# Sorted experts, two tiles at a time: shared PSUM banks for turned tiles and outputs, and twelve input places in place of sixteen

## The reference, cut to what matters

```python
for e in range(8):
    h = silu(flat @ W1[e]) * (flat @ W3[e])      # 128 -> 256
    out = out + cw[:, e:e + 1] * (h @ W2[e])     # 256 -> 128
```

## Time and profile before

| what | us |
|---|---|
| median of 3 runs | 2025.1 (2020.3 to 2026.32) |
| profiled execution, its own time | 2022.03 |
| span of its instructions | 2020.2 |
| m stage, from 1580 to 1718 | 138 |
| f stage, from 1853 to 1992 | 139 |

### The profile page before, as it was taken

One profiled execution on the slowest core, in us unless ns is written; L12 is line 12 of the kernel. 1 busy time (PEld: TensorE's weight loads), 2 busy tenths in 40 slices (PEclk: granted clock), 3 DMA queues, 4 the chain that ended last, 5 costly groups with the idle time before them and its releaser, 6 DMA issues. The chain is left out here.

```text
span 2020.2 us, 46758 instructions
## 1 busy us (share of the span) xinstructions
PE 1589.0 (79%) x16783; PEld 1166.6 (58%) x16783; DVE 1134.8 (56%) x3048; ACT 843.1 (42%) x1634; POOL 563.1 (28%) x782
## 2 busy tenths in 40 slices
PE   5788999999488879699988687898887597343992
PEld 3655666666266647478875454555554587332882
DVE  5745677777544447356544576876773343542433
ACT  2322455555211115344423254655553575001763
POOL 4111011111111103433202211133333355364554
PEclk9989799999699989899998886988896799555996
DMA  4000222221099200000001002222220242221224
GB/s 172 1 2 9 65 56 61 54 55 43 12 298 323 78 0 1 1 4 3 3 3 64 1 1 63 66 68 67 67 67 19 73 115 75 79 62 43 78 78 143
DMA packets 84683, 124.99 MB, mean 62 GB/s; under 512 B 17328, under 2 KB 70576, under 8 KB 82928
## 3 DMA queue, kind: packets, MB, share of 16 engines
q1 hardware_dynamic: 75824, 104.30, 17.7%
q0 software_dynamic: 8640, 17.78, 2.5%
HBM read 67.47 MB, written 55.59 MB: 61 GB/s over the span
## 5 line engine op out<-in xcount | busy, mean ns | idle before, releaser
L1527 DVE TENSOR_REDUCE small<-ps 128x8 f32<-128x1024 f32 (+1 forms) x256 | 312.6, 1223 | 122.6 <-PE ps L1313 70.4
L1454 ACT ACTIVATE scr<-ps 128x1024 f32<-128x1024 f32 x256 | 262.0, 1023 | 239.7 <-PE ps L1288 121.4
L244 POOL TENSOR_TENSOR rstd<-vare,neghalf 128x4 f32<-128x4 f32 (+1 forms) x72 | 63.2, 878 | 544.9 <-DVE vare L223 544.5
L2826 POOL DMA_INDIRECT results<-scr x142 | 135.9, 957 | 143.6 <-DVE scr L2815 59.0
L1326 PE MATMUL ps<-scr 128*32 128x256 f32 x2048 | 175.1, 417 | 0.2 <-ACT scr L1454 0.2
L1275 PEld LDWEIGHTS ps<-scr_r 32*128 32x128 f32 x1024 | 82.7, 196 | 153.3 <-ACT scr L1454 84.1
L1275 PE MATMUL ps<-scr_r 32*128 32x256 f32 x1024 | 137.0, 346 | 32.2 <-ACT scr L1454 18.4
L2746 PE MATMUL ps<-scr 128*128 128x128 f32 x1136 | 153.6, 279 | 1.3 <-ACT scr L2773 1.3
L1306 PE MATMUL ps<-scr_r 32*128 32x256 f32 x1024 | 138.6, 353 | 9.9 <-DMA scr_r<-scr_r 5.4
L2746 PEld LDWEIGHTS ps<-scr 128*128 128x128 f32 x1136 | 141.9, 196 | 1.6 <-issue 1.6
L1911 PE MATMUL ps<-scr 64*64 64x64 f32 x4480 | 120.8, 223 | 14.7 <-DVE scr L2201 7.0
(11 more groups left out here) (410 smaller groups left out, 3542.0 us busy)
## 6 DMA issues: line engine op xcount, KB each, us to landing
scr_r<-scr_r SPq DMA_DIRECT2D x512, 64.0 KB
rows_m<-kinds SPq DMA_DIRECT2D x8, 2064.0 KB, 30.3
rows_f<-kinds SPq DMA_DIRECT2D x8, 2064.0 KB, 74.3
scr<-results SPq DMA_DIRECT2D x32, 256.0 KB
scr<-rows_m SPq DMA_DIRECT2D x71, 64.5 KB
scr<-rows_f SPq DMA_DIRECT2D x71, 64.5 KB
scr<-in_l3m SPq DMA_DIRECT2D x1, 3072.0 KB, 9.9
results<-scr POOLq DMA_INDIRECT x142
```

Source lines behind the costliest of these rows:

```text
L244: pool.tensor_tensor(k.rstd[:, 0:self.J], k.vare[:, 0:self.J], k.neghalf[:, 0:self.J], ALU.pow).then_inc(self.e["rstd_ready"].sem, 1)
L1454: act.activation(PT[:, g % 2, 2 * x:2 * x + 2, :], ps[:, 4:6, :], ACT.Exp).then_inc(e["prob_ready"].sem, 1)
L1527: dve.tensor_reduce(nf[:, half, 0:blocks, at:at + 2].rearrange("p q a -> p a q"), ps[:, 2 * (p % 2):2 * (p % 2) + 2, :].rearrange("p a (q ...
L2826: pool.indirect_dma_start(results, bass.IndirectOffsetOnAxis(ap=names[:, j % IN, P:P + 1], axis=0), y[:, j % OUT, :], None).then_inc(store ...
```

## The change

Tiles 2m and 2m+1 form pair m. Turned tiles of a pair lie side by side in one bank (two banks), and ACT copies both by one instruction. Outputs of a pair lie side by side in one bank (two banks), and DVE copies both by one instruction. The products get four banks in place of three. `xT` and `y` get eight places in place of four. `xin` gets twelve places (`IN`) in place of sixteen. PE turns tile j+5 in step j in place of j+4. DVE copies pair m out behind the multiply of tile 2m+4, and POOL's two scatters of a pair wait for that copy.

```diff
-    IN, OUT, DEEP = 16, 4, 4
+    IN, XT, DEEP, OUT = 12, 8, 4, 8
     def turned_at(j):
-        return ps[:, j % 3, 0:P]
+        return ps[:, j // 2 % 2, P * (j % 2):P * (j % 2) + P]
     def hidden_at(j):
-        return ps[:, 3 + j % 3, :]
+        return ps[:, 2 + j % 4, :]
     def out_at(j):
-        return ps[:, 6 + j % 2, 0:P]
+        return ps[:, 6 + j // 2 % 2, P * (j % 2):P * (j % 2) + P]
     def sp(sp):
...
-            wait(sp, "turned", j - IN)
+            if there(j - IN):
+                wait_pair(sp, "turned", (j - IN) // 2)
             landed(sp, j - IN)
             arrived(sp, j - 4)
         def turn(j):
             arrived(pe, j)
-            wait(pe, "xt_ready", j - 3)
+            if j % 2 == 0:
+                wait_pair(pe, "xt_ready", j // 2 - 2)
...
         def gate_up(j):
-            wait(pe, "h_ready", j - 3)
+            wait(pe, "h_ready", j - 4)
...
         def project(j):
-            wait(pe, "out_read", j - 2)
+            if j % 2 == 0:
+                wait_pair(pe, "out_read", j // 2 - 2)
...
-        for j in range(-4, SORTED + 3):
+        for j in range(-5, SORTED + 3):
             if there(j):
                 gate_up(j)
-            if there(j + 4):
-                turn(j + 4)
+            if there(j + 5):
+                turn(j + 5)
             if there(j - 3):
                 project(j - 3)
...
+        def write_out(m):
+            wait(dve, "out_ready", tiles_of(m).stop - 1)
+            for j in range(2 * m - OUT, 2 * m - OUT + 2):
+                landed(dve, j)
+            out = ps[:, 6 + m % 2, 0:width(m)].rearrange("p (n c) -> p n c", c=P)
...
+        for j in range(SORTED + 5):
+            if ends_pair(j - 4):
+                write_out((j - 4) // 2)
             if there(j):
                 wait(dve, "act_ready", j)
...
-            wait(pool, "out_read", j)
+            wait_pair(pool, "out_read", j // 2)
             landed(pool, j - 4)
```

More of the change, by code:

```diff
@@ L2700, in wait, with wait_pair @@
             eng.wait_ge(e[name].sem, e[name].at(j))
+    def wait_pair(eng, name, m):
+        if 0 <= m:
+            eng.wait_ge(pairs[name].sem, pairs[name].at(m))
     def landed(eng, j):
@@ L2708, in arrived, with ends_pair, tiles_of, width @@
             eng.wait_ge(loads[j % 4].sem, loads[j % 4].at(j // 4))
+    def ends_pair(j):
+        return there(j) and (j % 2 == 1 or j == SORTED - 1)
+    def tiles_of(m):
+        return slice(2 * m, min(2 * m + 2, SORTED))
+    def width(m):
+        return P * (tiles_of(m).stop - 2 * m)
     def turned_at(j):
-        return ps[:, j % 3, 0:P]
+        return ps[:, j // 2 % 2, P * (j % 2):P * (j % 2) + P]
     def hidden_at(j):
-        return ps[:, 3 + j % 3, :]
+        return ps[:, 2 + j % 4, :]
     def out_at(j):
-        return ps[:, 6 + j % 2, 0:P]
+        return ps[:, 6 + j // 2 % 2, P * (j % 2):P * (j % 2) + P]
     def sp(sp):
@@ L2746, in gate_up @@
                     ins = pe.matmul(hidden_at(j)[:, 256 * n + P * c:256 * n + P * c + P],
-                                    here[:, j % DEEP, n, P * c:P * c + P], xT[:, j % DEEP, :], start=True, stop=True)
+                                    here[:, j % DEEP, n, P * c:P * c + P], xT[:, j % XT, :], start=True, stop=True)
             ins.then_inc(e["gu_ready"].sem, 1)
@@ L2773, in keep_weights, with keep_turned @@
             act.activation(here[:, j % DEEP], gate_up_of[:, :, bass.ds(at, 256)], ACT.Copy).then_inc(e["kept"].sem, 1)
-        def keep_turned(j):
-            wait(act, "turned", j)
-            wait(act, "gu_ready", j - DEEP)
+        def keep_turned(m):
+            wait_pair(act, "turned", m)
+            wait(act, "gu_ready", 2 * m + 1 - XT)
+            dst = xT[:, 2 * m % XT:2 * m % XT + width(m) // P, :].rearrange("p n c -> p (n c)")
+            src = ps[:, m % 2, 0:width(m)]
             if affine:
-                ins = act.activation(xT[:, j % DEEP, :], turned_at(j), ACT.Identity, scale=affine[0], bias=affine[1])
+                ins = act.activation(dst, src, ACT.Identity, scale=affine[0], bias=affine[1])
             else:
-                ins = act.activation(xT[:, j % DEEP, :], turned_at(j), ACT.Copy)
-            ins.then_inc(e["xt_ready"].sem, 1)
-        for j in range(-3, SORTED):
+                ins = act.activation(dst, src, ACT.Copy)
+            ins.then_inc(pairs["xt_ready"].sem, 1)
+        for j in range(-4, SORTED):
             if j == 2:
@@ L2788, in act @@
                 d.gap_exps(act)
-            if there(j + 3):
-                keep_turned(j + 3)
+            if ends_pair(j + 4):
+                keep_turned((j + 4) // 2)
             if there(j):
@@ L2799, in dve @@
         d.shift(dve)
-        for j in range(SORTED + 3):
+        def write_out(m):
[3 more added lines that the diff above has]
+            out = ps[:, 6 + m % 2, 0:width(m)].rearrange("p (n c) -> p n c", c=P)
+            dst = y[:, 2 * m % OUT:2 * m % OUT + width(m) // P, :]
+            if scale is None:
+                ins = dve.tensor_copy(dst, out)
+            else:
+                ins = dve.tensor_tensor(dst, out, row4(scale, width(m) // P), ALU.mult)
+            ins.then_inc(pairs["out_read"].sem, 1)
+        for j in range(SORTED + 5):
             if j == 4:
@@ L2809, in dve @@
                                   ALU.mult).then_inc(e["h_ready"].sem, 1)
[L2810 to L2818, removed]
             if beside and j < TILES:
@@ L2827, in pool @@
                                     y[:, j % OUT, :], None).then_inc(stores[j % 4].sem, 16)
-        for j in range(SORTED - OUT, SORTED):
+        for j in range(SORTED - 4, SORTED):
             landed(pool, j)
```

13 lines of the change are left out of this document (8 added, 5 removed).

## The result

The changed kernel takes 2116.5 us (median of 4 runs, 2095.3 to 2123.8), the kernel before beside it 2025.7 (4 runs, 2020.3 to 2029.4). The ratio is 1.043, with a 95% interval of 1.039 to 1.047. The direction was right. The size was not: 2062 was predicted, and 2116 lies above the range of 2038 to 2091.

The account below looks back on a forecast made before the run. No engine was full; PE's stall at the projection, then SP's loads, set the pitch. Twelve places at 1.94 us per tile added 18.5 (f) and 20.6 (m), 39 us on 2022.0: 2061, stated as 2062, range 2038 to 2091.

Parts of the forecast that it names:

- The mechanism: Both stages: twelve input places return too late, at 1.84 to 2.1 us per tile, 2041 to 2084 us; chance 0.70.
- Rival 2: Both stages: places are no limit, pairs remove PE's stall at the projection, 25 us less, 1998; chance 0.05.
- rival 1: Both stages: ring of places with late signals and slow SP, 2.2 us per tile, 2091; chance 0.13.
- Sum 7.36 us: Even tile's loop from projection through copy, scatter, landing, load and turning: four tiles, at least 1.84 us per tile.
- add 0.4 us: 7.76 / 4 = 1.94: Allowance for late PE signals on the loop of four tiles, giving the likeliest pitch, 1.94 us per tile.
- 0.11 + 0.45 + 1.45: PE's part of the loop: from turning to projection, that projection, then the next step to its projection's end; 2.01 us.
- 4 us for the pieces: Stage m: twelve 256 KB weight pieces ahead of loads on SP's queue; between 0 and 12 us, 4 taken.
- 58 tiles: Tiles per stage behind the first twelve, each charged the ring's pitch of 1.94 us in place of 1.655 or 1.689.
- The start: Each stage: the first copy-out waits for tile 1 and one more multiply; 2 us.
- Rival 3: Both stages: PE's clock falls to half for half of them, 50 us more, 2112; chance 0.08.
- 0.19 us per tile: PE's stall at the projection, 1.64 - 1.45, removed by pairs and the fourth product bank; 28 us at most.
- The range's upper end: Top of the ring case, 2084: 2.1 us per tile with the weight pieces in the loop.

Follow-up runs that it names:

- A: Changed kernel with sixteen input places in place of twelve and six turned places in place of eight: 1958.2 us, ratio 1.001 to the kernel before.
- B: Against the changed kernel (2106.9 us, ratio 1.040): table read ahead of the turning's wait, 2083.9, ratio 1.029; odd tiles' up-products computed twice, 2104.1, ratio 1.038.
- C: Changed kernel, still twelve places and pairs, with PE turning four tiles ahead in place of five: 2016.7 us, ratio 1.027 to the kernel before.
- the run with 0.96: Changed kernel with the two up-products of each odd tile computed twice by PE: 2104.1 us, ratio 1.038 to the kernel before.
- set E: Changed kernel with sixteen places and turnings four ahead, on a chip of 2034 us: 2052.3 us, ratio 1.010 to the kernel before.

## Why the prediction was right in direction and wrong in size

1. *The mechanism* was right: a place comes back after four tiles' loop through copy, scatter, landing, load, turning and projections. Sixteen places take the loss away (A), and two changes of one term each move the undisturbed loop by what the sum says: the read by 0.65 (B), the step of the turning by 1.65 (C). Rival 2 is out. Of rival 1, the 2.2 us per tile came true, but not its reason: of 30 copies in the middle of each stage none in f and one in m is over 1 us late, and five of 142 register instructions of SP's loads take over 0.1 us.
2. *The step that failed*: "Sum 7.36 us", then "add 0.4 us: 7.76 / 4 = 1.94". Undisturbed it measures 8.2. The term "0.11 + 0.45 + 1.45" = 2.01 measures 3.01. Of that, 0.74 is the 0.11, taken from an unblocked turning: the read of the table behind a blocked one makes it 0.85. The other 0.26 is in the 1.90 for the two projections and the step between them, which take 2.16 from the start of the first to the end of the second. The other terms stand within 0.1 and are 0.14 too long together. The 0.4 for late signals has nothing in its place: projection to copy is 0.24 in the median.
3. *The second failure is the greater one: the disturbances.* Over the 58 intervals that the ring binds the mean loop is 9.37 us in f and 9.40 in m, 1.2 above the undisturbed one. I had no term for this except 4 us for the pieces. A loop with no slack passes each late landing on. In 26 loops of f (pairs 3 to 28) the load comes 2.41 us behind the scatter at the best, 2.67 in the mean and up to 3.9. And idling brings short stretches at half clock, in which PE is the bound: in 7 of the 26 the part of 2.16 us takes 3.3 to 3.8, each time in such a stretch. The two runs of set B in which the clock came back agree: over the bound intervals f gained 8 us more than the read explains, and 8 us with the doubled products. In m the doubled products brought the clock from 0.93 to 0.96 and no time. How the rest divides was not measured apart.
4. *"58 tiles"* was the right number at the wrong end. The ring binds from the fifth scatter on, not from the thirteenth, since PE turns tile 12 before it projects tile 4; the first twelve intervals of f run at 2.26 us already. The last twelve are free of it, since nothing is loaded behind them.
5. *The start* was 2 us, it is 3.

The sum for f, from the predicted 18.5: the undisturbed loop (8.2 - 7.76) / 4 x 58 = 6.4, the disturbances (9.37 - 8.2) / 4 x 58 = 17.0, the start 0.8, the last twelve 12 x (1.72 - 1.655) = 0.8. That is 43.5, and 43.4 is measured. For m: 20.6 - 4 for the pieces, which the mean loop holds, + 6.4 + 17.4 + 0.9 + 2.4 = 43.7, as measured. So of the 25 us by which f was missed, a quarter is the mis-sized loop and two thirds are the missing term.

6. *Rival 3* (the clock) came true in part: 0.88 to 0.93 between the first and the last scatter of the stages with twelve places, below 0.9 in some of them, which was its sign. PE's busy time, which was to stay at 114 us, rose to 131 with it. But what it costs is some 8 us in f, not 50 in all, since PE would have waited in much of these stretches. The Trainium skill (TensorE: Matmul & The Clock Gate, "HAM oscillation") describes such swings with waits for DMA, and counts half of the throttled time as lost. The trace agrees on the first: PE waits for loads. The second is not borne out here, where PE is mostly not the bound: a mean of 0.88 over 156 us is 37 us at half clock, 0.96 over 150 us is 12. By that rule 19 and 6 us are lost, 13 less, and the run with 0.96 was 6 us shorter, with more products in it.
7. *PE's stall at the projection* did go, as said. But the 0.19 us per tile, counted as what pairs could gain, belonged to one chip's late signals. With sixteen places the pairs gain nothing on the fast chips (0.999 to 1.002) and lose 1% on the slow one, where only the version with turnings four ahead was run.
8. *The range's upper end* was summed without the later start: 58 x (0.445 + 0.411) + 12 + 4 is 66 us, 2088 and not 2084. The measured time lies beyond both.

No version here beats the kernel before beyond the intervals.

## What to carry to other kernels

Before places are taken from a ring, write out its loop, from the instruction that frees a place back to itself, and divide by the tiles that it moves on. That number is smaller than the number of places: here eight of them are held by tiles between turning and copy-out, and twelve places carry the loop by four tiles only. Each instruction queued behind the blocked wait belongs in the loop, register reads too; then leave room for disturbances, since a ring without slack hands every one on (9.4 us for 8.2 here, 14%). Batching two items into one copy lengthens the loop by the wait for the second, and which step of an in-order engine meets the freed place can be worth as much (1.65 of 8.2 us here). If a stall in one trace comes from signals that arrive late, look at a second chip before the stall is priced as the kernel's own.

## What the runs showed of the hardware that I had not expected

- On one chip PE's signals reach ACT and DVE late while PE runs without a stop (silus of f 1.26 us in the median with the kernel before, 2.7 in set E, 3.3 in the timeline shown), and SP's short instructions take up to 0.7 us; on a second chip, with the kernel before, a silu follows within 0.04 us, a copy within 0.24, and the instructions take 42 ns, and neither delay shows in the sixteen-place kernels on the two others. The two stages of the kernel before are 36 us longer on the first chip (118.6 + 116.5 for 98.6 + 100.6), and the rest of the program is 38 us longer in the two traces. The cause is open, a part of the recording in it included. Where PE stops every few us for the ring, the same chip shows next to nothing of either.
- A register read behind a blocked turning puts 0.65 us between the turning and the next matmul.
- In f of the changed kernel (set B) PE was idle for 36 of 156 us, in waits for loads of 1.2 us in the mean, and the granted clock fell to half in short stretches, 0.88 in the mean. It came back to 0.96 with 16% more matmuls (966 for 831).
- Four places of sixteen cost 0.9 to 1.7% in one order of the same work on fast chips, and in another 6.2% on a fast chip and 4.0% on the slow one.
